# Feed-forward of a fused window-attention, convolution and Fourier-mixer network: the next block's norm beside the own norm on the four quarters of TensorE

## The reference, cut to what matters

```python
def _ln_t(v, eps=1e-05):
    m = jnp.mean(v, axis=-1, keepdims=True)
    s = jnp.var(v, axis=-1, keepdims=True)
    return (v - m) / jnp.sqrt(s + eps)
...
x = _L0_conv_ref(x, ...)      # windows of 7x7, 3 heads, then an MLP with gelu
x = _L1_conv_ref(x, ...)      # norm, projection, 3x3 convolution, silu, residual
t = _to_tokens(x)
t = t + _L2_attn_ref(_ln_t(t), ...)   # projection, 2D Fourier transform, diagonal, inverse
t = t + _L2_ffn_ref(_ln_t(t), ...)    # relu(q(x) q(W1) + b1), then q(h) q(W2) + b2; q: fp8e5
t = t + _L3_attn_ref(_ln_t(t), ...)
t = t + _L3_ffn_ref(_ln_t(t), ...)
```

## Time and profile before

| | |
|---|---|
| median of three runs | 3321.04 us (3319.8 to 3326.78) |
| the profiled execution | 3324.36 us, of which the span of its instructions is 3322.6 us |
| mean granted TensorE clock | 0.971 of full speed |
| busy: PE, PEld | 2898.2 us (87%), 1838.1 us (55%) |
| busy: DVE, ACT, POOL | 1665.9 us (50%), 1611.3 us (48%), 363.6 us (11%) |
| matmul and weight-load instructions | 49148 each |

### The profile page before, as it was taken

One profiled execution on the slowest core, in us unless ns is written; L12 is line 12 of the kernel. 1 busy time (PEld: TensorE's weight loads), 2 busy tenths in 40 slices (PEclk: granted clock), 3 DMA queues, 4 the chain that ended last, 5 costly groups with the idle time before them and its releaser, 6 DMA issues.

```text
span 3322.6 us, 110007 instructions
## 1 busy us (share of the span) xinstructions
PE 2898.2 (87%) x49148; PEld 1838.1 (55%) x49148; DVE 1665.9 (50%) x2707; ACT 1611.3 (48%) x2899; POOL 363.6 (11%) x574
## 2 busy tenths in 40 slices
PE   6868889888899898998989989888898988988888
PEld 3536546466455573564744747447465474553754
DVE  5524546355553545544464445644457354572554
ACT  3542455533555425644266353563535535456245
POOL 4520010000100011001010011000110001100001
PEclk8989999999999999999999999999999999999999
DMA  2322000210001100110001100021000210001100
GB/s 80 69 59 52 2 16 5 53 33 2 17 16 50 25 2 17 32 51 6 2 18 42 46 1 2 18 54 34 1 2 19 54 34 1 2 19 34 33 1 16
DMA packets 28434, 84.79 MB, mean 26 GB/s; under 512 B 22002, under 2 KB 23138, under 8 KB 24114
## 3 DMA queue, kind: packets, MB, share of 16 engines
q1 hardware_dynamic: 26690, 72.55, 9.1%
q0 software_dynamic: 1280, 5.21, 0.6%
HBM read 61.70 MB, written 14.84 MB: 23 GB/s over the span
## 4 chain that ended last, share of the span: by engine, by line
PE 69%; ACT 13%; DVE 7%; issue 7%; SPq 3%; DMA 1%; ACTq 0%; DVEq 0%
PE ps L1128 69%; ACT lv L719 2%; SPq L495 2%; ACT area_ty L851 2%; ACT rs L724 2%; ACT sq L707 1%; DMA area_hz<-f_all 1%; DVE xs L1098 1%; DVE area_hz L979 1%; ACT area_hz L762 1%; ACT sq L705 1%; ACT area_ty L843 1%; DVE area_hz L996 1%; DVE area_ty L1094 1%; DVE area_ty L1070 1%
## 5 line engine op out<-in xcount | busy, mean ns | idle before, releaser
L1128 PE MATMUL ps<-area_hz 32*49 32x147 f32 (+3 forms) x7180 | 363.7, 288 | 89.2 <-DVE area_hz L979 24.1
L1128 PE MATMUL ps<-area_ty,area_hz 113*64 113x49 f32 (+2 forms) x10240 | 409.5, 256 | 8.8 <-ACT area_ty L741 8.1
L827 ACT ACTIVATE area_hz<-ps 121x384 f32<-121x384 f32 (+2 forms) x256 | 129.6, 519 | 583.5 <-PE ps L1128 583.5
L1128 PE MATMUL ps<-sq,keep_sb 64*64 64x392 f32 (+1 forms) x1728 | 340.2, 540 | 68.5 <-ACT sq L707 44.7
L1128 PEld LDWEIGHTS ps<-area_hz 32*49 32x49 f32 (+3 forms) x7180 | 290.2, 151 | 183.4 <-issue 160.9
L1128 PEld LDWEIGHTS ps<-area_ty,area_hz 113*64 113x64 f32 (+2 forms) x10240 | 319.4, 132 | 82.1 <-issue 80.9
L1128 PE MATMUL ps<-area_ty,g_sb 56*112 56x192 f32 (+1 forms) x3712 | 311.5, 321 | 26.0 <-DVE area_ty L1070 19.7
L1128 PEld LDWEIGHTS ps<-area_ty,g_sb 56*112 56x112 f32 x3712 | 293.0, 173 | 44.7 <-issue 44.0
L1128 PE MATMUL ps<-xs,keep_sb 64*64 64x448 f32 (+1 forms) x1184 | 217.2, 543 | 80.4 <-DVE xs L1098 49.7
L1070 DVE COPY area_ty<-ps 120x896 f32<-120x896 f32 (+1 forms) x192 | 164.8, 858 | 236.9 <-PE ps L1128 236.9
L719 ACT ACTIVATE lv<-ps 128x448 f32<-128x448 f32 (+1 forms) x304 | 158.6, 522 | 220.3 <-PE ps L1128 220.3
(11 more groups left out here) (124 smaller groups left out, 4325.7 us busy)
## 6 DMA issues: line engine op xcount, KB each, us to landing
area_hz<-f_all SPq DMA_DIRECT2D x16, 2541.0 KB
xw<-x_in SPq DMA_DIRECT2D x8, 1568.0 KB, 6.8
y_out<-xs SPq DMA_DIRECT2D x32, 252.0 KB
f_all<-piece POOLq DMA_DIRECT2D x16, 317.6 KB, 3.7
area_hz<-raw_in SPq DMA_DIRECT2D x1, 2894.0 KB, 9.4
g_sb<-g_in SPq DMA_DIRECT2D x6, 355.2 KB
area_ty<-area_hz SPq DMA_DIRECT2D x128, 9.2 KB
g_sb<-g_in SPq DMA_DIRECT2D x2, 710.5 KB
```

The lines of the kernel that those rows point to most:

```text
L827: act.activation(dst, src, ACT.Relu if st in (ST_H, ST_F2) else ACT.Copy).then_inc(sc_kept, 1)
L1128: return pe.matmul(o, a, b, start=start, stop=stop)
```

## The change

`together` pairs the two norms' products in the feed-forward: variance of own tile s-1 with variance of the side tile, center of own tile s with center of the side tile. The side norm uses PSUM bank 3 for both and has `side_sq`, `side_lv`, `side_rs` and six semaphores of its own. It lags three slots for l = 0 (`SIDE_LAG`), so that layer has eleven slots; `FFN_SLOTS` is NT + SIDE_LAG + 1 for both. Its last step is no longer a product of the centered tile in PSUM but of the uncentered tile in SBUF (`scale_side`); the centering is folded into `wq`, `wk` and `wv` once, in the setup (for `mix1` it already was). The own norm's centered tiles alternate between banks 0 and 1, and its center now stands before the down and up products. ACT's order in a slot becomes log own, log side, root own, root side, square own, square side, and then the copies of the down and up products. In `mlp` the filler `keep_busy(4, 1)` goes.

```diff
@@ sizes and banks
-FFN_SLOTS = NT + 3
+SIDE_LAG = 3
+FFN_SLOTS = NT + SIDE_LAG + 1
...
+def side_tile(l, i):
+
+    if l == 0:
+        return (LN_MIX(1), i) if 0 <= i < NT else None
+    return (LN_WIN1, i) if 0 <= i < NW else None
...
 def center_bank(k):
...
-    return {LN_MIX(1): 1, LN_WIN1: 1}.get(which, 0)
+    return i % 2
 def variance_bank(k):
...
-    return {LN_MIX(1): 3, LN_WIN1: 3}.get(which, 2)
+    return 2
@@ ScalarE, ffn
+                lag = 0 if l else SIDE_LAG
                 for s in range(FFN_SLOTS):
+                    done, new = side_tile(l, s - 1 - lag), side_tile(l, s - lag)
                     if 0 <= s - 1 < NT:
-                        invert(q, LN_FFN(l), s - 1)
-                    if l == 0 and 0 <= s - 3 < NT:
-                        invert(q, LN_MIX(1), s - 3)
-                    if l == 1 and 0 <= s - 1 < NW:
-                        invert(q, LN_WIN1, s - 1)
+                        log(q, LN_FFN(l), s - 1)
+                    if done:
+                        log_side(q, *done)
+                    if 0 <= s - 1 < NT:
+                        inverse_root(q, LN_FFN(l), s - 1)
+                    if done:
+                        root_side(q, *done)
+                    if s < NT:
+                        square(q, LN_FFN(l), s)
+                    if new:
+                        square_side(q, *new)
...
-                    if s < NT:
-                        square(q, LN_FFN(l), s)
-                    if l == 0 and 0 <= s - 2 < NT:
-                        square(q, LN_MIX(1), s - 2)
-                    if l == 1 and s < NW:
-                        square(q, LN_WIN1, s)
@@ VectorE
+            def scale_side(q, which, i):
+                w = ln_width(which)
+                ve.wait_ge(side_root, side_count(q, which, i))
+                o, a, b = xh[:, w * i:w * i + w], xw[:, w * i:w * i + w], side_rs[:, 0:w]
+                if which == LN_MIX(1):
+                    o = xhc[:, :, TR * i:TR * i + TR].rearrange("p w h -> p h w")
+                    a, b = (v.rearrange("p (h w) -> p h w", w=HW) for v in (xs[:, w * i:w * i + w], b))
+                ve.tensor_tensor(o, a, b, ALU.mult).then_inc(side_normed, 1)
...
-            ve.wait_ge(su_pe, 9)
+            ve.wait_ge(su_pe, 12)
...
+            su(ve.tensor_copy(wq[:, :], ps[:, 0, 384:512]))
+            su(ve.tensor_copy(wk[:, :], ps[:, 1, 384:512]))
+            su(ve.tensor_copy(wv[:, :, :], ps[:, 2, 0:4 * C].rearrange("p (j n) -> p j n", j=2)))
@@ TensorE, setup (norm)
+                mm(ps[:, 0, 384:512], K("center"), wq[:, :]).then_inc(su_pe, 1)
+                mm(ps[:, 1, 384:512], K("center"), wk[:, :]).then_inc(su_pe, 1)
+                pe.wait_ge(logged, ln_count(0, LN_AT[LN_FIRST, NW - 2]))
+                mm(ps[:, 2, 0:4 * C], K("center"), wv.rearrange("p j n -> p (j n)")).then_inc(su_pe, 1)
@@ TensorE, mlp
                         if i == 1:
-                            keep_busy(4, 1)
@@ TensorE, ffn
+                    if done:
+                        pe.wait_ge(side_squared, side_count(q, *done))
+                        across = (3, ln_width(done[0]), K("variance"), side_sq[:, 0:ln_width(done[0])])
                     if 0 <= s - 1 < NT:
-                        variance(q, LN_FFN(l), s - 1)
...
+                        along = (variance_bank(k), TT, K("variance"), sq[:, k % 2, 0:TT])
+                        if done:
+                            made, side = together(along, across)
+                            side.then_inc(side_var_made, 1)
+                        else:
+                            made = blocks(*along)
+                        made.then_inc(var_made, 1)
+                    elif done:
+                        crossed(*across).then_inc(side_var_made, 1)
...
-                    if l == 0 and 0 <= s - 3 < NT:
-                        variance(q, LN_MIX(1), s - 3)
-                    if l == 1 and 0 <= s - 1 < NW:
-                        variance(q, LN_WIN1, s - 1)
+                    if new:
+                        if l == 0:
+                            pe.wait_ge(ffn_added, q * 2 * NT + new[1] + 1)
...
+                        if new[1] >= 1:
+                            pe.wait_ge(side_logged, side_count(q, *new) - 1)
+                        w, x = ln_width(new[0]), xw if l else xs
+                        across = (3, w, K("center"), x[:, w * new[1]:w * new[1] + w])
+                    if s < NT:
...
+                        along = (center_bank(k), TT, K("center"), xs[:, TT * s:TT * s + TT])
+                        if new:
+                            made, side = together(along, across)
+                            side.then_inc(side_centered, 1)
...
-                    if s < NT:
-                        pe.wait_ge(ve_kept, q * VE_FILLS + vector_fills(step_of(l, ST_FFN, s) + 1))
-                        center(q, LN_FFN(l), s, xs)
-                    if l == 0 and s > NT:
+                    if l == 0 and NT < s < FFN_SLOTS - 1:
                         keep_busy(4, 1)
-                    if l == 0 and 0 <= s - 2 < NT:
-                        pe.wait_ge(ffn_added, q * 2 * NT + s - 1)
-                        center(q, LN_MIX(1), s - 2, xs)
-                    if l == 1 and s < NW:
-                        if s == 0:
-                            pe.wait_ge(x_loaded, q * 16 + 32)
-                        center(q, LN_WIN1, s, xw)
```

More of the change, by code:

```diff
@@ L118, in _tile_order @@
                 order.append((LN_FFN(l), s))
-            if l == 0 and 0 <= s - 2 < NT:
-                order.append((LN_MIX(1), s - 2))
-            if l == 1 and s < NW:
-                order.append((LN_WIN1, s))
     return order
@@ L134, in ln_count, with side_count @@
     return q * LN_N + NW + k + 1
+SIDE_N = NT + NW
+def side_count(q, which, i):
+    return q * SIDE_N + (i if which == LN_MIX(1) else NT + i) + 1
+def side_tile(l, i):
+    if l == 0:
+        return (LN_MIX(1), i) if 0 <= i < NT else None
+    return (LN_WIN1, i) if 0 <= i < NW else None
 def ln_width(which):
@@ L708, in square, with log @@
                                ).then_inc(squared, 1)
-            def invert(q, which, i):
+            def log(q, which, i):
                 k = LN_AT[which, i]
@@ L720, in invert, with inverse_root @@
                                    ).then_inc(logged, 1)
+            def inverse_root(q, which, i):
+                k = LN_AT[which, i]
+                w = PT if in_pairs(which) else ln_width(which)
                 if two_before(k):
@@ L725, in invert, with square_side, log_side, root_side @@
                                ).then_inc(root, 1)
+            def invert(q, which, i):
+                log(q, which, i)
+                inverse_root(q, which, i)
+            def square_side(q, which, i):
+                n, w = side_count(q, which, i), ln_width(which)
+                act.wait_ge(side_centered, n)
+                if n >= 2:
+                    act.wait_ge(side_var_made, n - 1)
+                act.activation(side_sq[:, 0:w], ps[:, 3, 0:w], ACT.Square).then_inc(side_squared, 1)
+            def log_side(q, which, i):
+                n, w = side_count(q, which, i), ln_width(which)
+                act.wait_ge(side_var_made, n)
+                act.activation(side_lv[:, 0:w], ps[:, 3, 0:w], ACT.Ln).then_inc(side_logged, 1)
+            def root_side(q, which, i):
+                n, w = side_count(q, which, i), ln_width(which)
+                if n >= 2:
+                    act.wait_ge(side_normed, n - 1)
+                act.wait_ge(side_logged, n)
+                act.activation(side_rs[:, 0:w], side_lv[:, 0:w], ACT.Exp, scale=-0.5).then_inc(side_root, 1)
             def norm(q, which):
@@ L1084, in ffn @@
                         scale(q, LN_FFN(l), s - 1, xq8[:, TT * (s - 1):TT * s], saturate=False)
-                    if l == 0 and 0 <= s - 3 < NT:
-                        scale_mix(q, 1, s - 3)
-                    if l == 1 and 0 <= s - 1 < NW:
-                        scale_windows(q, LN_WIN1, s - 1)
+                    done = side_tile(l, s - 1 - (0 if l else SIDE_LAG))
+                    if done:
+                        scale_side(q, *done)
                     if 0 <= s - 2 < NT:
@@ L1586, in ffn @@
             def ffn(q, l):
+                lag = 0 if l else SIDE_LAG
                 for s in range(FFN_SLOTS):
+                    done, new = side_tile(l, s - 1 - lag), side_tile(l, s - lag)
+                    if done:
+                        pe.wait_ge(side_squared, side_count(q, *done))
+                        across = (3, ln_width(done[0]), K("variance"), side_sq[:, 0:ln_width(done[0])])
                     if 0 <= s - 1 < NT:
-                        variance(q, LN_FFN(l), s - 1)
+                        k = LN_AT[LN_FFN(l), s - 1]
+                        pe.wait_ge(squared, ln_count(q, k))
+                        before = user_before(variance_bank, k)
+                        if before is not None:
```

(10 more changed lines are left out.)

42 lines of the change are left out of this document (27 added, 15 removed).

## The result

The changed kernel takes 3230.39 us (median of four runs, 3225.27 to 3234.65), the kernel before beside it 3323.91: a ratio of 0.9718, 95% interval 0.9698 to 0.9738. The forecast was 3217 with a range of 3203 to 3250. The change is worth 93.5 us; 104 were forecast.

What follows compares the result with a forecast made beforehand. Feed-forward in both layers held by a loop over several engines, none full. Eight quads of 7.3 + 5.1 (99.2), filler 7.6, minus setup 2.6: 104.2 off 3324.36 gives 3220.2; median, 3.3 lower, 3217 us, range 3203 to 3250.

Steps and rivals of the forecast that it cites:

- The slot: Feed-forward slot on TensorE: fill to center, center pair, down and up, variance pair; sum 4.79, taken as 4.85 us.
- from the start of the fill to the start of the center 1.76: First part of the slot: the fill plus DVE's addition that center needs, priced at 1.76 us.
- ACT's log, tight but under: Feed-forward slot: the next side center needs the side log, ready at 4.6 us, under TensorE's 4.79.
- Four quarters cost what two do: Feed-forward pairs: two norms' products on four quarters hold TensorE 0.90 us, the same as a group of two.
- some 0.9 longer: Own norm's centered tile: with one bank the next center waits for the scale, lengthening a slot some 0.9 us.
- The tail: Last fill of layer one to the mixer's first product: chain stays, 1.1 us a quad saved from 21.5.
- Layer two: Second layer's feed-forward, first to last fill: 35.0 becomes 29.9 us, a gain of 5.1 a quad.
- granted clock 1.00 within the feed-forward: Sign that the prediction is right: TensorE's granted clock stays at 1.00 throughout the feed-forward.
- 8 either way: Range allowance for a slow stretch more or less in some quads: 8 us in either direction.
- The filler: Removed filler in the MLP, in a chain through the norm to the gelu copies: 0.95 us a quad, 7.6 in all.
- the rival with a chance of 0.09: Filler's place is colder: without it a further slow stretch may follow in each quad, 14 us more, 3231; chance 0.09.
- The setup: Once, ahead of the first keys: three products and three copies more, +2.6 us, between +1 and +4.

Runs made afterwards that it cites:

- the control: The changed kernel itself run again with nothing altered, as base for its series: 3235.93 us, ratio 0.9735 to the kernel before.
- the side log test: Against the changed kernel, ACT takes the side norm's log ahead of the own one in each feed-forward slot: 3227.51 us, ratio 0.9716 to the kernel before.
- series one: Four kernels on one chip: changed kernel again, filler restored, side log first, filler behind layer two's first center pair; ratios 0.9735, 0.9752, 0.9716, 0.9725 to the kernel before.

## Why the prediction was right, and where it was off

The number lies within its range, 13 us above the forecast, and the mechanism is the one forecast: the pairs on four quarters, with the two banks and the center in front. By terms it is less exact than by the sum. In the profiled execution the windows themselves, layer one and layer two, gave 15.9 us less than forecast, and the terms around them 11.1 more. In the control, the same kernel, the terms around gave 2.5 less than forecast, so that surplus is luck. The range was drawn narrowly too: its own bounds, added up one by one, reach 3196 to 3235, not 3203 to 3232.

- **The slot.** Taken as 4.85; measured 4.87 in the second layer and 5.06 in the first in the slots with a side log. A pair takes 0.92 for 0.90, down and up 336.23 - 335.00 = 1.23 for 1.23. The step that failed is "from the start of the fill to the start of the center 1.76": that row is of a slot without the side norm. It is 1.82 in the second layer, where the side norm puts one wait more in front of the center, but 339.14 - 337.15 = 1.99 in the first, where it puts two. With one of them gone, layer one is 0.34 shorter: 8 x 0.34 = 2.7 us of the 3.6 that its term lacks.
- **The other loops.** "ACT's log, tight but under": the side log test shows that it holds nothing. The cast ends at 339.78 and down starts at 340.06: it fits by 0.28, 0.2 was forecast. I overlooked the loop over ACT and DVE (center, squares, down's copy, L1145, L1149, L1156, L1133, center); it happens to be as long as TensorE's, so missing it cost nothing, by luck.
- **Four quarters cost what two do.** Right: 0.92. Issue in turn or not is the same, and without them nothing is gained. The Trainium skill (TensorEngine Tiling (Array Packing), "Restrictions and Gotchas", Gotcha 1) would have forbidden two row tiles at once in one bank; no trace here shows a cost of it.
- **The second bank and the place of center.** The forecast named the bank ("some 0.9 longer" with one; measured 0.6 to 1.0 in undisturbed gaps). The center's new place it took as given and did not price. Each is needed: undoing any one of the three parts, quarters, bank or place, takes the whole gain away.
- **The tail.** Forecast 1.1. From the last fill of layer one to the mixer 21.48 became 368.03 - 347.27 = 20.76, 0.7. Over the eight quads the tail gives 10.1 for the 8.8 forecast, since three quads of the kernel before had 1.4 to 1.6 more in it; the other 4.2 of the 14.3 lie in the mixer, which the change doesn't touch. The side scale takes 0.93 (L1020), the upper bound, where I took 0.75 "nearest in kind".
- **Layer two.** The term's size is right where the clock stays up: 4.9 a quad for 5.1. Three slow stretches took 10.5 of its 12.3 missing us. The sign "granted clock 1.00 within the feed-forward" was not met. The prediction checked the clock only for steady slots and gave slow stretches no term, only "8 either way" in the range. The falls at layer two's start are of two kinds. In the kernels with all three parts and no filler there, 21 of 64 quads have one. In 11 it comes 2.0 to 2.4 us behind the first fill, ahead of the third idle time; in 10 it comes 3.7 to 4.4 behind it, at the end of that idle time or after. The second kind has the pairing's new idle time in front of it. The first kind has in front of it in this stage only what the kernel before has as well, and there it came in none of eight quads; why, is open. That both fillers together removed both kinds (none of eight), and the second filler alone made the first kind shorter, fits this but is one profile each.
- **The filler.** Its own price, 0.95, is exact at full clock, which two of eight quads had. In sum over the stage it costs 9.0 in series one, for 7.6. Whether the place is colder without it, the rival with a chance of 0.09, the totals don't show.
- **The setup.** First keys at 43.67 before and 46.29 now: +2.6, as forecast. To the first fill it is +2.9.

What stays open: how the waits turn into time, why the clock falls in some quads and not in others that read alike, and what the fillers at layer two's start are worth over many executions.

## What to carry to other kernels

When work of a side stream is laid beside the main one, look at the slots in which the loop fills up: there the pair leaves TensorE idle, and two cheap fillers in idle times can give back more than trimming the steady slot did (15.6 us against a kernel that had many slow stretches, 6 to 11 against the changed kernel, which the intervals don't settle; trimming gave about 3 by the gaps). Read where a clock fell in order of time before blaming the idle time that is new: here half of the falls came ahead of it. Write down every loop of the new slot engine by engine, DVE's order too, and price a hand-over from a slot with the same waits in front. If three edits each shorten one loop of the same slot, taking out any one of them can take the whole gain; adding one alone was not run here.

## What the runs showed of the hardware that I had not expected

- A wait on TensorE that was fulfilled long before still lengthened the hand-over behind it: 0.10 us with three waits in a row, 0.26 or 0.27 with four. Two waits gave 0.06 or 0.15, depending on which two.
- The clock fell to its 1.2 GHz level at the start of layer two, around idle times of only 0.81, 0.84 and 1.02 us, with a fill and a center group between them: in 21 of 64 quads over the eight profiled executions with all three parts and no filler in that place, in none of 8 in the one with two fillers. In 11 of the 21 it fell before the third idle time began.
- A filler that lies in the chain lengthened its piece by its own time, 0.95 us, where the clock was up (6.05 for 5.10). Where the clock was down the piece was no longer than the slowest without it, and the time was lost further on.
